# Second pass of a two-layer sequence kernel: the output product moved by one step, the expert chosen in four operations, and the log-sigmoids split

## The reference, cut to what matters

```python
q1 = x @ Wq * scale ; k1 = x @ Wk ; v = x @ Wv
q2 = x @ Wqa @ Wqb * scale ; k2 = softmax(x @ Wka @ Wkb)         # per head
gk1 = log_sigmoid(x @ Wg1a @ Wg1b + bg1) / 16                    # first decay
gk2 = log_sigmoid(x @ Wg2a @ Wg2b + bg2) / 16                    # second decay
mask = one_hot(argmax(x @ We))                                   # 1 of 4 experts per row
o = gla(q1, k1, v, gk1) + sum over e of gla(q2*fac_e, k2*fac_e, v, gk2*mask_e)
g = x @ Wga @ Wgb
o = o * rsqrt(mean(o*o) + eps) * norm_w                          # per head
y = (o * (g * sigmoid(g))) @ Wo
out = x + layernorm(y)
```

## Time and profile before

| | |
|---|---|
| three runs | 2893.90, 2894.51, 2912.56 us, median 2894.51 |
| profiled execution | 2894.36 us, span 2892.5 us |
| mean granted TensorE clock | 0.976 of 2.4 GHz |
| busy | PE 2608.7, PEld 1613.3, DVE 1987.7, ACT 1695.4, POOL 923.6 us |

### The profile page before, as it was taken

How to read it: one execution, slowest core, us unless ns; L and a number is a source line. 1 busy time by engine, 2 the same in 40 slices (tenths; PEclk the granted TensorE clock), 3 DMA queues, 4 the chain that set the end, 5 groups by cost and what they waited for, 6 DMA issues and landing times.

```text
span 2892.5 us, 55901 instructions
## 1 busy us (share of the span) xinstructions
PE 2608.7 (90%) x20208; PEld 1613.3 (56%) x20208; DVE 1987.7 (69%) x4006; ACT 1695.4 (59%) x3345; POOL 923.6 (32%) x750
## 2 busy tenths in 40 slices
PE   6999799989999999999779997998999999999987
PEld 3444466555655666655534444655566665655654
DVE  4442487788777777877644425778877787777786
ACT  4332566666666666666434325666666666666664
POOL 2884222223322233222212241222333223322222
PEclk9999899999999999999889998999999999999999
DMA  5120100000000000000022101000000000000000
GB/s 186 59 90 33 37 23 22 22 22 22 27 25 25 22 22 22 22 22 22 19 88 62 62 32 35 23 22 22 22 22 28 26 22 22 22 22 22 22 22 12
DMA packets 48376, 97.49 MB, mean 34 GB/s; under 512 B 5376, under 2 KB 5376, under 8 KB 47680
## 3 DMA queue, kind: packets, MB, share of 16 engines
q1 hardware_dynamic: 37008, 68.44, 7.3%
q10 hardware_dynamic: 9792, 17.83, 1.7%
q0 software_dynamic: 1520, 10.50, 0.9%
HBM read 63.19 MB, written 33.55 MB: 33 GB/s over the span
## 4 chain that ended last, share of the span: by engine, by line
PE 66%; DVE 23%; issue 7%; ACT 4%; DMA 0%; DVEq 0%; ACTq 0%; SPq 0%
PE psum L303 12%; PE psum L304 11%; PE psum L305 11%; PE psum L581 6%; DVE region L1147 5%; PE psum L437 5%; PE psum L454 4%; PE psum L427 4%; DVE region L1203 4%; PE psum L473 3%; DVE region L1212 2%; DVE region L1144 2%; DVE og L1091 2%; DVE og L1272 2%; DVE region L1223 1%
## 5 line engine op out<-in xcount | busy, mean ns | idle before, releaser
L1007 POOL TENSOR_TENSOR region<-region,kfac 128x512 f32<-128x512 f32 x64 | 66.8, 1043 | 769.1 <-DVE kfac L1231 769.1
L303 PE MATMUL psum<-wb,region 128*128 128x512 f16 x768 | 292.4, 381 | 4.1 <-DVE region L1203 4.1
L304 PE MATMUL psum<-wb,region 128*128 128x512 f16 x768 | 292.5, 381 | 0.0
L305 PE MATMUL psum<-wb,region 128*128 128x512 f16 x768 | 292.3, 381 | 0.0
L995 POOL TENSOR_TENSOR region<-region 128x1024 f32<-128x1024 f32 x64 | 150.2, 2347 | 430.6 <-DVE region L1116 430.6
L990 POOL TENSOR_TENSOR region<-region 128x1024 f32<-128x1024 f32 x64 | 146.5, 2290 | 288.8 <-DVE region L1354 230.7
L1002 POOL TENSOR_SCALAR region<-region,m 128x512 f32<-128x512 f32 x256 | 172.9, 695 | 180.7 <-DVE hm L1184 104.4
L1354 DVE SCALAR_TENSOR_TENSOR region<-psum,region 128x512 f16<-128x512 f32 x64 | 44.3, 692 | 262.0 <-ACT region L830 262.0
L498 PE MATMUL psum<-ident,og 128*128 128x128 f16 x512 | 42.2, 229 | 171.4 <-DVE og L1091 171.4
L1147 DVE SCALAR_TENSOR_TENSOR region<-psum,m,region 128x256 f32<-128x256 f32 x384 | 185.8, 484 | 13.7
L716 ACT ACTIVATE region<-region 128x1024 f16<-128x1024 f32 x64 | 67.7, 1058 | 197.9 <-DVE region L1203 197.9
(11 more groups left out here) (235 smaller groups left out, 7841.8 us busy)
## 6 DMA issues: line engine op xcount, KB each, us to landing
region<-x_in SPq DMA_DIRECT2D x128, 256.0 KB, 2.7
q_cols<-region ACTq DMA_DIRECT2D x64, 256.0 KB, 2.3
region<-q_cols SPq DMA_DIRECT2D x64, 256.0 KB, 2.9
out_rows<-region SPq DMA_DIRECT2D x60, 256.0 KB, 2.0
region<-wb_in POOLq DMA_DIRECT2D x1, 3072.0 KB, 11.8
region<-wqkv_in SPq DMA_DIRECT2D x4, 512.0 KB, 5.6
region<-wqkv_in POOLq DMA_DIRECT2D x2, 1024.0 KB, 5.7
region<-wproj_in POOLq DMA_DIRECT2D x2, 1024.0 KB, 7.5
```

The costliest lines, as they stand in the source:

```text
L303: mm(out, lhs(0), rhs(0), start=start, stop=False)
L304: mm(out, lhs(0), rhs(1), start=False, stop=False)
L305: return mm(out, lhs(1), rhs(0), start=False, stop=stop)
```

## The change

- `og_transpose` and `out_mm` work on tile t = n - 2 in place of m = n - 1, at the same places of PE's order. So do `back_og`, `back_norm3` (ACT), `back_out` (DVE) and the store (SP). Each pass has one more step. DVE runs `back_norm`, `back_normed`, `back_gated` and `back_split` of tile m later in the step: the norm after `sil`, the others after the gated queries, and the split last before the residual of tile n + 1. `back_rms` goes behind the exponentials of the decays on ACT. The residual with its mean is kept in a buffer of its own (`xr`), made at the end of ACT's step.
- `back_select` has four operations on 128x512 in place of eight on 128x256, and waits for all eight products of the expert states. `project_k2` and `project_k`, which write banks 3 and 2, wait for the fourth.
- Abs, Exp, Ln and the log-sigmoid are made on 128x1024 for the decays and then on 128x512 for the output gate. On ACT the row of labels is built ahead of the copy of the values.
- Loads are one tile earlier against the stores.

```diff
 # PE
             def project_k2(n, back):
                 pe.wait_ge(S("carry_ok"), prev(n))
                 if back:
-                    pe.wait_ge(S("sel_ok"), (n - 1) * 8 + 4)
+                    pe.wait_ge(S("sel_ok"), (n - 1) * 4 + 4)
...
-                for half, done in ((0, "ia_pe"), (1, "ib_pe")):
-                    if half and front:
+                for half in (1, 0):
+                    if half == 0 and front:
                         pe.wait_ge(S("v_ok"), cur(n + 1))
...
-                    last.then_inc(S(done), 1)
-                pe.wait_ge(S("out_ok"), prev(n))
+                last.then_inc(S("ix_pe"), 1)
+                if not front:
+                    pe.wait_ge(S("out_ok"), n)
...
-            def og_transpose(n):
+            def og_transpose(n, back):
                 pe.wait_ge(S("og_ok"), cur(n))
+                if back:
+                    pe.wait_ge(S("osum_ok"), cur(n + 1))
...
+                m, mp, t = n - 1, 1 - p, n - 2
...
-                if back:
-                    og_transpose(m)
+                if tail:
+                    og_transpose(t, back)
                 if front:
                     project_q2(n)
                     cumulate(n, back)
-                if back:
-                    out_mm(m)
+                if tail:
+                    out_mm(t)
 # ACT, order of step
                     front_low(n)
+                    front_label(n)
                     front_v(n, p)
-                    front_label(n)
-                    front_gates(n, 0)
+                    front_gates(n)
                     front_router(n)
-                    front_gates(n, 1)
+                    front_decays(n)
+                    front_swish(n)
                     front_sig_high(n)
                 if back:
                     back_square(m)
-                    back_rms(m)
...
-                if back:
-                    back_og(m)
+                if tail:
+                    back_og(t)
                 if front:
                     front_exps(n)
                 if back:
-                    back_norm3(m)
+                    back_rms(m)
+                if tail:
+                    back_norm3(t)
...
+                if front:
+                    front_residual(n, p, tail)
 # DVE
-                for half in range(2):
-                    dve.wait_ge(S(("ia_pe", "ib_pe")[half]), cur(n))
...
+                dve.wait_ge(S("ix_pe"), cur(n))
+                to = osum.rearrange("p (h d) -> p h d", h=H2)
+                of = psum[:, 0:4, :].rearrange("p b (r e d) -> p (b r) e d", r=2, e=NEXP)
+                ve.tensor_scalar(to, of[:, :, 0, :], m4[:, p, 0:1], None, ALU.mult).then_inc(S("sel_ok"), 1)
+                for e in range(1, NEXP):
+                    dve.wait_ge(S("sel_ok"), n * 4 + e)
+                    ve.scalar_tensor_tensor(to, of[:, :, e, :], m4[:, p, e:e + 1], to, ALU.mult, ALU.add).then_inc(S("sel_ok"), 1)
```

More of the change, by code:

```diff
@@ L283, in _ @@
                     load(j0, p)
-                with sp.Fori(b * (TILES // 2) + 1, b * (TILES // 2) + TILES // 2) as j:
+                for p in range(2):
+                    wait_alone(sp, S("x1_ok"), j0 * 2 + 2 + p)
+                    wait_alone(sp, S("qz_ok"), j0 * 2 + 2 + p)
+                    load(j0 + 1, p)
+                with sp.Fori(b * (TILES // 2) + 2, b * (TILES // 2) + TILES // 2) as j:
                     for p in range(2):
@@ L288, in _ @@
                         load(j, p)
-                        store(j - 1, p)
+                        store(j - 2, p)
+                for p in range(2):
+                    store(j0 + TILES // 2 - 2, p)
             for p in range(2):
@@ L505, in out_mm, with step @@
                 last.then_inc(S("wo_pe"), 1)
-            def step(n, p, front=True, back=True, ahead=True):
-                m, mp = n - 1, 1 - p
+            def step(n, p, front=True, back=True, tail=True, ahead=True):
+                m, mp, t = n - 1, 1 - p, n - 2
                 if front:
@@ L541, in step @@
                 if ahead:
-                    xn_transpose(n + 1)
+                    xn_transpose(n + 1, back)
                 if front:
@@ L624, in _ @@
                 xn_transpose(n0, again=False)
[L625 to L628, removed]
+                step(n0, 0, back=False, tail=False)
+                step(n0 + 1, 1, tail=False)
+                with pe.Fori(b * TILES + 2, b * TILES + TILES - 2, 2) as n:
+                    step(n, 0)
+                    step(n + 1, 1)
+                step(n0 + TILES - 2, 0)
                 step(n0 + TILES - 1, 1, ahead=False)
                 step(n0 + TILES, 0, front=False, ahead=False)
+                step(n0 + TILES + 1, 1, front=False, back=False, ahead=False)
         @block.scalar
@@ L757, in back_square @@
                 act.wait_ge(S("osum_ok"), cur(n))
-                act.wait_ge(S("og_ok"), prev(n))
-                ac(osq[:, :], osum, ACT.Square).then_inc(S("osq_ok"), 1)
+                act.wait_ge(S("oms_ok"), prev(n))
+                ac(osq, osum, ACT.Square).then_inc(S("osq_ok"), 1)
             def back_rms(n):
@@ L892, in _ @@
                 ahead_full(n0, 0)
[L893 to L896, removed]
+                step(n0, 0, back=False, tail=False)
+                step(n0 + 1, 1, tail=False)
+                with act.Fori(b * TILES + 2, b * TILES + TILES - 2, 2) as n:
+                    step(n, 0)
+                    step(n + 1, 1)
+                step(n0 + TILES - 2, 0)
                 step(n0 + TILES - 1, 1, ahead=False)
                 step(n0 + TILES, 0, front=False, ahead=False)
+                step(n0 + TILES + 1, 1, front=False, back=False, ahead=False)
                 for p in range(2):
@@ L1282, in back_out, with step @@
                 dve.wait_ge(S("x1m_ok"), cur(n))
-                ve.scalar_tensor_tensor(ob[:, p, :], bank[7], rstd[:, 2, :], x1[:, p, :], ALU.mult, ALU.add).then_inc(S("out_ok"), 1)
-            def step(n, p, front=True, back=True, ahead=True):
-                m, mp = n - 1, 1 - p
+                ve.scalar_tensor_tensor(ob[:, p, :], bank[7], rstd[:, 2, :], xr[:, p, :], ALU.mult, ALU.add).then_inc(S("out_ok"), 1)
+            def step(n, p, front=True, back=True, tail=True, ahead=True):
+                m, mp, t = n - 1, 1 - p, n - 2
                 if back:
@@ L1299, in step @@
                     front_masks(n)
+                if front:
+                    front_prob(n)
                 if back:
@@ L1307, in step @@
                 if front:
+                    front_logsig3(n)
                     front_kmax(n)
+                    front_kdiff(n)
+                    front_lslow(n)
+                    front_kfac(n)
+                    front_sil(n, p)
                 if back:
                     back_norm(m)
[L1311 to L1320, removed]
                 if ahead:
@@ L1407, in _ @@
                 ahead_low(n0, 0)
[L1408 to L1411, removed]
+                step(n0, 0, back=False, tail=False)
+                step(n0 + 1, 1, tail=False)
+                with dve.Fori(b * TILES + 2, b * TILES + TILES - 2, 2) as n:
+                    step(n, 0)
+                    step(n + 1, 1)
+                step(n0 + TILES - 2, 0)
                 step(n0 + TILES - 1, 1, ahead=False)
                 step(n0 + TILES, 0, front=False, ahead=False)
+                step(n0 + TILES + 1, 1, front=False, back=False, ahead=False)
 def layouts(i):
```

95 lines of the change are left out of this document (53 added, 42 removed).

## The result

The changed kernel takes 2748.2 us (median of four runs, 2746.39 to 2748.74) against 2897.74 before: ratio 0.9474, 95% interval 0.9439 to 0.9509. The forecast was 2744 in 2718 to 2800. The profiled execution took 2748.56 us, its span is 2746.7.

A forecast was written before the change was run, and what follows sets the result against it. PE waits each step for DVE's chain from selection to split. 58 x 2.23 = 129.3, second steps 8.7, last ones 6.2, clock 17.9, less drains 11.2: 150.9 us off 2894.51, so 2744 us, range 2718 to 2800.

The forecast's parts named there:

- The hole ahead of the transposes: PE's 2.73 us wait at L498 for DVE's split goes; L498 comes 2.23 us earlier, so does the step's end.
- The row of labels: Built ahead of the values on ACT, it lets PE's L473 start behind the carry, 0.26 us earlier.
- The hole ahead of L365: New 0.76 us PE wait ahead of the key projections (L357 before) for the selection's end; bounds 0.3 to 1.7.
- The selection: On DVE, four operations take 3.1 us and end at 1022.42; PE's key projections start 0.50 us later.
- Slack of DVE: DVE ends its step's work 1.2 us before the residual is due; held by POOL's L1018 alone, just in time.
- The rival in which POOL's second operation gets in ahead of the split: L1019 also delays DVE's split, residual 1.9 us late in 60 steps: 2856 us; chance 0.06 without clock.
- The clock: Eleven steps of about 36.0 us, slowed behind the hole ahead of L498, return to 34.31: 17.9 us gained.
- The rival that a hole of 0.8 us brings the clock down: PE's clock still falls as often, behind the new 0.76 us hole or others: 2762 us; chance 0.10.
- The sum: All terms over both passes: 150.9 us gained, from 2894.51 to 2743.5, given as 2744.
- The second step: Without an output product in each pass's second step, PE gains 2.23 + 2.1 us; 8.7 for two.
- The ends of the passes: The two last front steps gain 6.2 us together; the two drains cost 2 x 5.6.
- The drain's extra chain: Tile 30's copy, norm, product and output ahead of the last split end each pass 5.6 us later.

The follow-up runs named there:

- Experiment 8: Changed kernel with the selection by halves, one log-sigmoid for all gates and the values ahead of the row of labels on ACT: 2722.61 us, ratio 0.9366.
- experiment 1: Changed kernel with the selection by halves, eight operations on 128x256, key projections waiting for the first half only: 2705.28 us, ratio 0.9326.
- Experiment 2: Changed kernel with DVE's split of the gated output put behind the residual of the next tile: 2749.98 us, ratio 0.948.
- Experiment 9: Changed kernel with the selection by halves and DVE's carry made half by half in PE's order: 2696.46 us, ratio 0.9285.
- Experiment 4: Kernel before with eight more matmuls, result unread, in PE's hole ahead of the transposes of the gated output: 2872.55 us, ratio 0.9904.
- Experiment 5: Kernel before with the selection in four operations alone, waiting for all eight products: 2872.23 us, ratio 0.9884.
- experiments 6 and 7: Kernel before, one part each: row of labels ahead of the values on ACT, 2900.7 us, ratio 0.9994; log-sigmoids apart, 2860.86 us, ratio 0.9844.
- experiment 10: Changed kernel with selection and carry by halves, split behind the residual, router's exponential ahead of the row of labels: 2679.75 us, ratio 0.9234.

## Why the prediction was right

**The hole ahead of the transposes.** Right in place and size. From the first low-rank matmul of the step L509 came at 17.41 us where L498 came at 19.62: 2.21 earlier, 2.23 forecast. Experiment 8 shows that the move of the product alone closes it.

**The row of labels.** Forecast 0.26, measured 0.15: PE starts its fp32 products 0.25 us behind the end of the carry, not 0.15. That term was sized from no row that showed it. The hole ahead of L365 is smaller for it: 0.64 us by the pace of the matmuls, 0.76 forecast.

**The selection.** The four operations take 0.75, 0.77 each with their waits, 3.1 in all as forecast. L365 comes 0.50 later against the start of the step, exactly as said. By the figure in the Trainium skill, VectorE: DVE Perf Modes, in its TRN2 errata, they would be estimated at 0.66 each; the rows decided rightly. What the prediction did not say plainly is that this part loses: it had 0.50 of PE's time as a cost against nothing gained, and experiment 1 has it at 0.65 a step, 0.50 for the later L365 and 0.15 for what the earlier row of labels gains.

**Slack of DVE.** Forecast 1.2 us without the port, and just in time with it. Measured 0.20 to 0.28 us, with both stalls (0.3 and 0.73) in place; the split's second part takes 1.42, not the 1.7 forecast. The rival in which POOL's second operation gets in ahead of the split did not come: the split ends 0.55 behind L1051 while L1052 follows, so the held DVE operation goes first. The rule of the Trainium skill, SBUF — State Buffer, section Who interferes with whom, holds for the lock, in all of L1302, L1124 and L1052. The prediction says that the section does not tell who comes next; it does say that issue order decides who blocks, and the trace agrees, with the split started at 989.64 and L1052 at 990.48. Experiment 2 shows that the stall costs nothing here. Experiment 9 has it on the path once PE's holes are closed; what it costs there was not measured by itself.

**The clock.** Eleven long steps were to vanish and did. Experiment 4 shows the cause. Experiment 5 shows that it is the hole in one piece: nearly the same idle time in two pieces gives no long step. The rival that a hole of 0.8 us brings the clock down is out for the full steps, by those after and those of experiment 4. It is not out everywhere. In the second step of a pass the clock does fall in some runs, though the changed kernel's profile has none there. In experiment 1's first pass it fell at 375.1, behind these two holes, and that step took 31.85 us at a granted clock of 0.95; its second pass has the same two holes, 30.75 us and 1.00.

```profile
373.65 0.20 PE L424 MATMUL psum<-halves,region 128*128 128x2 f16 x2 [0.88 <-ACT region L761]
...
374.76 0.39 PE L326 MATMUL psum<-bias,ones 128*128 128x512 f16 x1 [0.56 <-DVE region L1124]
```

**The sum.** Forecast 150.9 us, measured 145.8 between the two spans. From tile 0's row of labels to tile 31's on PE (L352, L360) the passes lose 72.8 and 73.4 us, 146.3 together, against 155.9 forecast for that stretch. A full step gave 2.15, not 2.23 (4.6 us in all: the label, and 0.06 behind L509): this is the largest miss, with that of the ends. The second step gave 3.5 and 3.6, not 4.3 (1.5), since PE waits 0.88 us for ACT ahead of L424 there. The first step was not in the sum and got 1.2 and 2.2 us longer, at a granted clock of 0.89 for 0.94 and 1.00. That much is not fixed by the kernel: in experiment 1 the same step takes 30.25 us at 0.89 in one pass and 27.47 at 1.00 in the other. The ends of the passes, with all else outside that stretch, were forecast to lose 5.0 and lost 0.5. The drain's extra chain is 3.4 and 3.6 us (join to output 14.25 and 14.09 before, 17.62 and 17.66 after), not 5.6. In the last drain the first of its two output products ran at the higher clock, with matmuls 0.22 us apart where the second has 0.43, which is 2.5 us for twelve; that this is the difference is my estimate. The errors stood against each other, so the total is nearer than its parts, and that is luck.

## What to carry to other kernels

Where PE waits in each step for a chain of another engine that ends in a product for the output, let that product work on the tile before: it needs another buffer and one more step, and gives back the whole wait if the other engine still ends in time. Saving operations on DVE by waiting for a larger input of PE's can cost more than it saves; start on the first half of what PE makes and free the first half for it. When PE's holes are closed, look at what each remaining wait hides: one edit here gave nothing alone and another 0.3%, and with a third they gave 0.9% (2705 to 2680 us).

## What the runs showed of the hardware

- A DVE operation with two SBUF inputs beside the POOL operations of these rows is held to the end of the one that runs (1.42 and 0.98 us for 0.69), and then goes ahead of the next one in POOL's queue, which takes 2.35 us. Where the split was moved away (experiment 2) that one takes 1.91 again. DVE's cast to fp16 is stretched beside POOL as well: 0.54 to 0.62 us for 0.42 in experiment 2, 0.68 to 0.86 in experiment 10.
- The granted clock can fall now and then (in 11, 18 and 11 of 60 steps: the kernel before, experiments 6 and 7) at holes of PE of 2.05 to 2.56 us that come back every step. Each of these falls began at the end of such a hole, from 0.5 us ahead of it to 1.4 behind, and cost 1.4 to 1.7 us. It fell in no full step where the largest hole was 1.88 or 0.83 (experiments 5 and 4), but it did in a second step with holes of 0.88 and 0.56 (experiment 1). Matmuls whose result is unread in the hole (experiment 4) or a hole in two parts (experiment 5) are worth 1.0 to 1.2% of this kernel.
